# A delta-rule attention layer with an 8-expert MoE: block inverses from 16x16 halves, VectorE transposes, and expert tiles of 256 rows

## The reference

```python
kb = k * beta[..., None]
att = jnp.where(tri, 0.0, -(kb @ jnp.swapaxes(k, -1, -2)))        # strictly lower, 32 x 32 a chunk
for i in range(1, chunk):                                         # the inverse of I - att, row by row
    upd = jnp.einsum('bhnj,bhnjk->bhnk', att[..., i, :], att)
    att = att.at[..., i, :i].add(upd[..., :i])
att = att + jnp.eye(chunk)
u, w = att @ v, att @ kb                                          # v is beta * v
def step(S, xs):                                                  # over the chunks
    u_adj = u_i - w_i @ S
    o_i = q_i @ S + local @ u_adj
    return S + jnp.swapaxes(k_i, -1, -2) @ u_adj, o_i
...
gout = x @ Wgate + bgate                                          # top 2 of 8 experts
z = (x @ W1 + b1) * (x @ W2 + b2)                                 # 128 -> 256
g = z @ Wg + bg                                                   # 256 -> 256
o = g * sigmoid(g) * (z @ Wl + bl)
y = o @ W3 + b3                                                   # 256 -> 128
return x + attention + sum of the two experts' y by their shares
```

## Time and profile before

| | us |
|---|---|
| median of 3 runs (lowest to highest) | 948.98 (945.25 to 949.86) |
| the profiled execution | 941.82 |
| its span, first to last instruction | 939.9 |
| PE busy / PE weight loads | 674.9 / 524.2 |
| DVE busy | 677.4 |
| POOL busy | 467.7 |
| ACT busy | 272.5 |
| DMA | 113.04 MB, 120 GB/s over the span |
| mean granted clock of PE | 0.791 |

### The profile page before, as it was taken

One profiled execution on the slowest core, in us unless ns is written; L12 is line 12 of the kernel. 1 busy time (PEld: TensorE's weight loads), 2 busy tenths in 40 slices (PEclk: granted clock), 3 DMA queues, 4 the chain that ended last, 5 costly groups with the idle time before them and its releaser, 6 DMA issues.

```text
span 939.9 us, 33031 instructions
## 1 busy us (share of the span) xinstructions
PE 674.9 (72%) x14332; PEld 524.2 (56%) x14332; DVE 677.4 (72%) x1432; ACT 272.5 (29%) x489; POOL 467.7 (50%) x526
## 2 busy tenths in 40 slices
PE   3762855757886879589877787777888887676651
PEld 3552853546564656467666565656666575555531
DVE  5769988876955898678658895897477973894241
ACT  2432113241342234222522332233144223113020
POOL 2622137782444556335824783274723257753635
PEclk9855557798977898777978899899796987566575
DMA  9765545374315223701531537326542124213121
GB/s 346 277 249 195 166 159 190 107 201 128 101 26 156 87 81 82 153 26 58 175 114 41 138 109 211 99 59 155 109 106 81 43 87 104 78 49 105 34 71 56
DMA packets 87598, 113.04 MB, mean 120 GB/s; under 512 B 57312, under 2 KB 62432, under 8 KB 83360
## 3 DMA queue, kind: packets, MB, share of 16 engines
q0 software_dynamic: 11616, 51.03, 18.8%
q1 hardware_dynamic: 68720, 37.50, 14.5%
q10 hardware_dynamic: 7120, 22.42, 6.7%
HBM read 77.63 MB, written 34.90 MB: 120 GB/s over the span
## 4 chain that ended last, share of the span: by engine, by line
PE 34%; DVE 26%; issue 16%; POOL 10%; DMA 5%; SPq 4%; ACT 4%; ACTq 1%; DVEq 0%; POOLq 0%
PE ps_shared L1581 6%; DVE solve_prod L1435 5%; PE ps_shared L1737 4%; PE ps_shared L1799 4%; PE ps_g L1577 3%; SPq L842 3%; PE ps_l L1577 3%; DVE solve_T L1442 3%; POOL xs L994 3%; PE ps_shared L1577 3%; PE ps_shared L1716 2%; PE ps_shared L1586 2%; DMA solve_L<-system_d 2%; DVE acc L1364 2%; PE ps_x L1577 2%
## 5 line engine op out<-in xcount | busy, mean ns | idle before, releaser
L1435 DVE TENSOR_TENSOR solve_prod<-solve_T,solve_L 128x2 f32<-128x2 f32 (+30 forms) x248 | 129.7, 523 | 35.7 <-DMA solve_L<-system_d 29.8
L994 POOL DMA_INDIRECT xs<-xn_d,owner_i x92 | 91.7, 997 | 50.5 <-issue 24.9
L1060 POOL TENSOR_TENSOR z<-work,z 128x512 fp32r<-128x512 f32 x46 | 59.5, 1294 | 98.7 <-ACT z L1229 98.4
L1442 DVE TENSOR_REDUCE solve_T<-solve_prod 128x1 f32<-128x2 f32 (+30 forms) x248 | 101.0, 407 | 6.2
L1577 PE MATMUL ps_x<-xr,w_up 128*128 128x512 f32 x276 | 94.8, 459 | 7.3 <-DVE work L1544 4.4
L1577 PE MATMUL ps_g<-z,w_mid 128*128 128x512 f32 x276 | 85.2, 448 | 10.5 <-DVE work L1548 5.6
L1577 PE MATMUL ps_l<-z,w_mid 128*128 128x512 f32 x276 | 79.4, 425 | 0.2 <-DVE work L1553 0.2
L1026 POOL DMA_INDIRECT w_mid<-y_d,slot_i x64 | 63.4, 991 | 18.4 <-issue 17.9
L1799 PE MATMUL ps_shared<-w_mid,work 128*128 128x128 f32 x368 | 56.3, 317 | 21.9 <-DVE work L1553 18.2
L1577 PEld LDWEIGHTS ps_g<-z,w_mid 128*128 128x128 f32 x276 | 55.8, 210 | 28.4 <-issue 13.2
L1737 PE MATMUL ps_shared<-head_vs,taps 32*32 32x16 f32 x4096 | 54.9, 196 | 20.3 <-issue 19.3
(11 more groups left out here) (246 smaller groups left out, 1428.5 us busy)
## 6 DMA issues: line engine op xcount, KB each, us to landing
mid_d<-w_mid ACTq DMA_DIRECT2D x8, 1024.0 KB, 5.8
work<-expert_weights ACTq DMA_DIRECT2D x16, 384.0 KB, 4.4
y_d<-work SPq DMA_DIRECT2D x23, 256.0 KB, 2.2
xa_d<-xr SPq DMA_DIRECT2D x8, 512.0 KB, 6.7
xa<-xa_d SPq DMA_DIRECT2D x8, 512.0 KB, 4.3
up_d<-w_up ACTq DMA_DIRECT2D x8, 512.0 KB, 3.0
solve_L<-system_d SPq DMA_DIRECT2D x64, 64.0 KB
system_d<-masked SPq DMA_DIRECT2D x8, 256.0 KB, 3.4
```

What stands on the lines that cost most here:

```text
L994: pool.indirect_dma_start(xs[par][:, c, :], None, xn_d.rearrange("w p (c d) -> (w p c) d", c=CPW), bass.IndirectOffsetOnAxis(owner_i[:, w ...
L1060: pool.tensor_tensor(low[:, :], up1[i], high[:, :].bitcast(FP), ALU.subtract).then_inc(S["z_low"], 1)
L1435: seq.mark(dve.tensor_tensor(prod, solve_T[:, 0:k, 0:i + 1], over(solve_L[:, i, 0:i + 1].unsqueeze(1), P, k, i + 1), ALU.mult))
L1442: made = dve.tensor_reduce(solve_T[:, 0:k, i], prod, AX.X, ALU.add, negate=True)
```

## The change

1. **The solve** takes only the two 16 x 16 triangles on the diagonal of each block, 128 of them on 128 partitions: 15 steps of i x i elements. `solve_in` is 8 DMAs of 16 x 16 x 16, `inverse_out` is 1 DMA, `inv` is 8 DMAs into `parts`, a block-diagonal tile. Two new stages make the lower left quarter, -D2 x L x D1 in the block's terms: `low` (PE, 64 small products of 16 columns; DVE transposes `parts` into `parts_T`; ACT copies the product to `low_part` with a scale of -1 or 0 by partition), and `full` (PE, 64 small products; DVE copies the first 16 columns of `parts` to `inverse` and adds the product to the other 16). `system` on POOL, `eye` and the diagonal are gone. `u` waits for `full`.
2. **Beta and router rows** are turned by one DVE transpose a window of 32 x 32 blocks (`by_step`); ACT takes the sigmoid from there; `rank` is 4 additions of 32 partitions. ACT's copy, the 64 one-column products and the router's 4 transposes on PE are gone. Wgate is laid out for each of the four heads.
3. **Experts** in tiles of 256 rows: the formula for TILES gives 39 instead of 23 (9984 slots, not 11776). Both halves j share one bank, 256 columns each, and a stage does both: 36 matmuls of 256 columns a tile as before of 512, `down` 4 fp32 products (8 before), 2 row gathers and 2 transposes (4 before). `load_up` and `load_mid` are one each a tile as before, so 39 each. DVE's and ACT's bias steps are two of 128 x 256 a stage; `zlow` and ACT's copy of z stay 128 x 512, one a tile. The load streams are split in even and odd tiles.
4. `FLOW` and `PULL` are set anew, so the order of the work changes everywhere.

```diff
-TILE = 512
+TILE = 256
 TILES = (2 * SEQS * STEPS + EXPERTS * (TILE - 1)) // TILE
 SLOTS = TILES * TILE
 CHUNKS = WINDOWS * CPW
-LANES = TILES * CPW
+CPT = TILE // P
+LANES = TILES * CPT
+MOST = SEQS * STEPS // TILE
 MARK = 8
...
-        return [[(DVE_, 0.1 + min(i, KH) * (i + 1) / 900)]]
+        return [[(DVE_, 0.14 + i * i / 900)]]
...
-        yield need(("solve_in", w, 0))
-        for i in range(1, CHUNK):
+        yield need(("masks0", 0, 0), ("solve_in", w, 0))
+        for i in range(1, KH):
             yield "solve_mul", w, i, None
             yield "solve_sum", w, i, None
         if w >= 2:
...
         yield need(("inverse_out", w, 0))
         if w == 0:
             yield "fold", 0, 0, None
+        yield "inv", w, 0, None
         if w:
             yield need(("w_T", w - 1, 1))
-        yield "inv", w, 0, None
+        bk = yield TAKE
+        yield "low", w, 0, bk
+        leave(bk, "low", w + 1)
+        bk = yield TAKE
+        yield "full", w, 0, bk
+        leave(bk, "full", w + 1)
         yield need(("v_b", w, 0), ("k_T", w, 0))
         if w >= 1:
...
-        yield need(("own", 0, 0) if kind == "load_xs" else ("image_out", EXPERTS - 1, 0), ("place", 0, 0))
-        for t in range(TILES):
+    def expert_loads(kind, par, behind):
...
+                elif name == "inv":
+                    sp.wait_ge(S["in_inverse"], 16 * (w + 1))
+                    sp.wait_ge(S["masked"], 1)
+                    if w:
+                        sp.wait_ge(S["full"], w)
+                        sp.wait_ge(S["low_ps"], w)
+                        sp.wait_ge(S["parts_T"], w)
                     for half in range(2):
-                        sp.dma_start(inverse_d[par, :, KH * half:KH * half + KH, :],
-                                     solve_T[64 * half:64 * half + 64, :, :]).then_inc(S["in_inverse"], 16)
-                elif name == "inv":
-                    sp.wait_ge(S["in_inverse"], 32 * (w + 1))
-                    if w:
-                        sp.wait_ge(S["wT_ps"], w)
-                    for h in range(HEADS):
-                        sp.dma_start(inverse[head_rows(h), :, :],
-                                     inverse_d[par, h * RUNS:h * RUNS + RUNS].rearrange("n k i -> k n i")).then_inc(
-                                         S["in_inv"], 16)
+                        for h in range(HEADS):
+                            first = HD * h + KH * half
+                            sp.dma_start(parts[first:first + KH, :, KH * half:KH * half + KH],
+                                         inverse_d[par, half, h * RUNS:h * RUNS + RUNS].rearrange("n k i -> k n i")).then_inc(
+                                             S["in_inv"], 16)
                 elif name == "x_res":
                     if w:
                         sp.wait_ge(S["in_part"], 16 * w)
                     else:
-                        sp.wait_ge(S["beta_T"], WINDOWS)
...
+                elif name == "beta":
+                    dve.wait_ge(S["rows_ps"], w + 1)
+                    if w >= 2:
+                        dve.wait_ge(S["beta"], w - 1)
+                        dve.wait_ge(S["glog"], w - 1)
+                    dve.transpose(by_step[par], runs_flat(ps[:, :])).then_inc(S["rows"], 1)
...
                 elif name == "solve_mul":
-                    k = min(i, KH)
-                    prod = solve_prod[:, 0:k * (i + 1)].rearrange("p (k j) -> p k j", k=k)
+                    prod = solve_prod[:, 0:i * i].rearrange("p (k j) -> p k j", k=i)
                     if i == 1:
                         dve.wait_ge(S["in_solve"], 16 * SOLVE_LOADS * (w + 1))
-                        dve.wait_ge(S["eye"], w + 1)
+                        dve.wait_ge(S["masked"], 1)
+                        if w:
+                            dve.wait_ge(S["in_inverse"], 16 * w)
                     else:
                         dve.wait_ge(seq.sem, summed_at)
-                    seq.mark(dve.tensor_tensor(prod, solve_T[:, 0:k, 0:i + 1],
-                                               over(solve_L[:, i, 0:i + 1].unsqueeze(1), P, k, i + 1), ALU.mult))
+                    seq.mark(dve.tensor_tensor(prod, solve_T[:, 0:i, 0:i],
+                                               over(solve_L[:, i, 0:i].unsqueeze(1), P, i, i), ALU.mult))
                     product_at = seq.n
                 elif name == "solve_sum":
-                    k = min(i, KH)
-                    prod = solve_prod[:, 0:k * (i + 1)].rearrange("p (k j) -> p k j", k=k)
+                    prod = solve_prod[:, 0:i * i].rearrange("p (k j) -> p k j", k=i)
                     dve.wait_ge(seq.sem, product_at)
-                    made = dve.tensor_reduce(solve_T[:, 0:k, i], prod, AX.X, ALU.add, negate=True)
-                    if i < CHUNK - 1:
+                    made = dve.tensor_reduce(solve_T[:, 0:i, i], prod, AX.X, ALU.add, negate=True)
+                    if i < KH - 1:
...
+                elif name == "low":
+                    dve.wait_ge(S["in_inv"], 16 * SOLVE_LOADS * (w + 1))
+                    if w:
+                        dve.wait_ge(S["full_ps"], w)
+                    dve.transpose(parts_T[:, :, :], parts[:, :, :]).then_inc(S["parts_T"], 1)
+                elif name == "full" and not halfway:
+                    halfway = True
+                    if w:
+                        dve.wait_ge(S["wT_ps"], w)
+                    dve.tensor_copy(inverse[:, :, 0:KH], parts[:, :, 0:KH])
+                elif name == "full":
+                    halfway = False
+                    dve.wait_ge(S["full_ps"], w + 1)
+                    dve.tensor_tensor(inverse[:, :, KH:], ps[:, 0:RUNS * KH].rearrange("p (r i) -> p r i", i=KH), parts[:, :, KH:],
+                                      ALU.add).then_inc(S["full"], 1)
                 elif name == "fir" and i:
                     if i == 1:
...
+                    dve.wait_ge(S["up1"], w + 1)
+                    dve.wait_ge(S["x2"], w + 1)
+                    for j in range(FJ):
+                        own = half(up1[par], j)
+                        made = dve.scalar_tensor_tensor(own, half(ps_x2, j), bias_of(1, w, j), own, ALU.add, ALU.mult)
+                    made.then_inc(S["z"], 1)
...
+                elif name == "low":
+                    pe.wait_ge(S["in_inv"], 16 * SOLVE_LOADS * (w + 1))
+                    pe.wait_ge(S["system_raw"], CPW * (w + 1))
+                    for r in range(RUNS):
+                        for h in range(HEADS):
+                            made = small(ps, KH * r, KH, h, masked[par][head_rows(h), r // SEQS, 0, r % SEQS, :],
+                                         parts[head_rows(h), r, KH:])
+                    made.then_inc(S["low_ps"], 1)
+                elif name == "full":
+                    pe.wait_ge(S["low"], w + 1)
+                    pe.wait_ge(S["parts_T"], w + 1)
+                    for r in range(RUNS):
+                        for h in range(HEADS):
+                            made = small(ps, KH * r, KH, h, parts_T[head_rows(h), r, :], low_part[head_rows(h), r, :])
+                    made.then_inc(S["full_ps"], 1)
                 elif name == "u":
-                    pe.wait_ge(S["in_inv"], 64 * (w + 1))
+                    pe.wait_ge(S["full"], w + 1)
                     pe.wait_ge(S["v_b"], w + 1)
-                    pe.wait_ge(S["k_b"], w + 1)
+                    pe.wait_ge(S["beta_mask"], w + 1)
                     for r in range(RUNS):
                         for h in range(HEADS):
                             made = small(ps, HD * r, HD, h, inverse[head_rows(h), r, :], v_b[par][head_rows(h), r, :])
...
+                elif name in ("mid_g", "mid_l"):
+                    n = int(name == "mid_l")
+                    if n == 0:
...
+                    for j in range(FJ):
+                        for k in range(FJ):
+                            made = product(half((ps_g, ps_l)[n], j), [gl_of(w, part, k, n, j) for part in range(2)],
+                                           [z[par][:, part, k, :] for part in range(2)], start=k == 0, stop=k == FJ - 1)
+                    made.then_inc(S[("g_ps", "l")[n]], 1)
                 elif name == "down":
-                    pe.wait_ge(S["o"], FJ * (w + 1))
-                    for c in range(CPW):
+                    pe.wait_ge(S["o"], w + 1)
+                    for c in range(CPT):
                         for k in range(FJ):
-                            made = pe.matmul(ps[:, c * D:(c + 1) * D], gated[par][k][:, c * P:(c + 1) * P], down_of(w, k),
+                            made = pe.matmul(ps[:, c * D:(c + 1) * D], half(gated[par], k)[:, c * P:(c + 1) * P], down_of(w, k),
                                              start=k == 0, stop=k == FJ - 1)
                     made.then_inc(S["y_ps"], 1)
```

415 lines of the change are left out of this document (193 added, 222 removed).

## The result

| | before | after |
|---|---|---|
| median (lowest to highest), us | 949.38 (945.25 to 949.86) | 979.72 (978.93 to 986.48) |
| profiled span, us | 939.9 | 977.4 |
| PE / DVE / POOL busy, us | 674.9 / 677.4 / 467.7 | 670.5 / 543.2 / 455.8 |
| DMA, MB | 113.04 | 134.56 |
| granted clock | 0.791 | 0.76 |

The changed kernel is slower: ratio 1.0345, 95% interval 1.029 to 1.040. On another chip it ran at 1.0149 (1.009 to 1.0207) of the kernel before, so the loss is 1.5 to 3.5 per cent. There two of its four runs, 975 and 993 us, were in a slower state and don't count, so that ratio rests on runs of 959 and 969 us. The forecast was 871.

A forecast was written before the change was run, and what follows sets the result against it. B was taken as PE work plus waits, half for a DVE 74% full; in C and D a chain decides. 177 + 547 + 52 + 86 = 862 of span, plus 1.9 and 7.2 for the median: 871; range 826 to 925.

The forecast's parts named there:

- A: Stretch from the start to window 0's u, 0 to 217 us before; forecast 177, bounds 165 to 195.
- B: Stretch from window 0's u to window 6's, 217 to 799 us before; forecast 547, bounds 510 to 600.
- C: Stretch from window 6's u to window 7's, 799 to 854 us before; forecast 52, bounds 45 to 60.
- D: Tail after window 7's u, 854 to 940 us before, without solve or experts; forecast unchanged at 86.
- Behind the solve: Path from the solve's output issue to u's products: 7.2 us before, forecast 15, or 16 with a SyncE queue gap.
- Experts: Expert matmuls in B: 256 columns cost 0.54 of 512, nothing gained or lost, -17 to +50 us at the ends.
- Rival 3: Short expert matmuls cost 0.66: B +50, time 921; slower than before from 0.73 on; chance 0.08, 0.02 for that end.
- PE busy in B: TensorE's work in B: 467.7 - 6 - 1 + 23 = 483 us.
- The clock: TensorE's granted clock in B rises from 0.86 to 0.90 with fewer gaps, taken as worth 15 us.
- Idle in B: TensorE's idle time in B: 31 for DVE, 25 issue, 15 rest, 8 new hand-offs, 79 us; 114 before.
- Rival 1: PE's waits for DVE in B are a chain's and stay: B 597, time 921; chance 0.20.
- Rival 4: Expert weight loads with two buffers set the tile's beat; at 17 us B is 629, time 953; chance 0.06.

The follow-up runs named there:

- all three at once: Changed kernel, own order, with low and full products for one run only, half the expert weight bytes and one load for the solve's input: 887.1 us, 0.934.
- Few products: Changed kernel, own order, with low and full products of the last run alone, 4 instead of 64 in each: 940.63 us, 0.9912.
- half the weights: Changed kernel, own order, with half the bytes in each expert weight load, 0.89 MB a tile instead of 1.78: 939.42 us, 0.9919.
- the same new order: Kernel before laid out anew by its planner with trace durations and a searched preference table, first order: 1.0025; slower chip 1.0017.

## Why the prediction was wrong

It forecast 871 and faster; the kernel is 1.5 to 3.5 per cent slower. Of the 115 us of span that are missing, A has 13, B 86 (68 of idle time, 15 of clock, 3 of work), C 14 and D 2.

- *The solve's own steps*: right. 38.9 + 28.7 = 67.6 us, where 68 were said. *Small products' busy time*: right, 28.4 against 30.
- *Behind the solve*, 15 us, "hand-offs 0.5": mis-sized. Window 0's solve ends at 160.0 and its inverse is complete at 185.3: 25. Some 7 us of it are the two stalls inside low and full, the loads start 4.4 us after the output is issued (2.2 in window 7 before), and the eight loads land 3.4 us behind their last issue.
- *Stretch A*, 177: 190. The solve ended 25 us after it began, as forecast; 12 of the 13 us are the path behind it, with u itself. With the stalls and traffic cut (all three at once) A is 175.
- *Experts*, ratio 0.54: right, 0.166 / 0.315 = 0.53. Rival 3 and its far end fall. On the line through the 81 and 131 ns of the Trainium skill (TensorE: Matmul & The Clock Gate, Back-to-back issue gap) the ratio would be 0.75, an estimate; the trace doesn't agree, at 0.53. DVE's pairs were dearer than the 838 ns I took from a plain product: each half takes 475, a pair 950 (L1585, L1578 and L1572 alike), so the split costs 0.2 a pair and not 0.09, 24 us in all. That part of an instruction's time is fixed, as the Trainium skill has it (VectorE: DVE Perf Modes, The TRN2 errata), agrees with the trace, 950 for two halves against 745; how much of the 24 us PE waited for isn't separated.
- *PE busy in B*, 483: right, 486. *The clock*, 15 us: didn't come; it was 0.83 and not 0.90, beside 147 us of gaps where 79 were forecast.
- *Idle in B*, 79: this is the step that failed; it is 147. Two of its terms were wrong. Of the 61 us that DVE released I kept 31, "since its load falls"; it is 58. DVE's load did fall, by 86 us, but load was not what the waits hung on: in the new order DVE stands for the solve's loads, whose trip takes 9.2 to 15.6 us where the order was laid for 7.1, and one load in place of eight gave 12 us back. Of the 37 of "issue" I kept 25, while the change adds 1500 instruction pairs to PE and 28 MB to the queues from which it is supplied; it is 63. That row was in front of me, with "issue" as its largest line, and I priced low and full at the busy time of their like, though a group of the like has its own row of waits: L1581 in the earlier trace rows has 11.0 us of issue beside its 15.2 of work. Few products and half the weights, 22 us less each, are the two cuts at this term, and both went with shorter issue waits.
- *C*, 52: 66; *D*, 86: 88. "With 30 steps it is done long before" held the order of the triangles fixed, and it moved.
- *Rival 1* had the mechanism nearest to it: PE's waits stay, and DVE's did, 58 against 61. It was too small, as it didn't let issue grow. *Rival 4*, weight loading as the tile's beat, is not what happened: the loads land in 7.4 us, PE waits 7.7 us for them in B. But 35 MB less gave 22 us, with PE's issue waits 21 us shorter, and that no rival had; what the 28 MB more of the change cost by themselves wasn't measured.

## What to carry to other kernels

A group of small instructions costs its supply too: put the "issue" idle of the like beside its busy time, and look at what the change adds to the DMA queues in the same stretch. Where engines run fixed lists, work that is taken off one engine only pays if the list doesn't send it to its next wait early: check the landings that the order was laid with against the trace, before and not after the table of preferences is tuned. And a part can't be judged in one order; two orders of the same stages were up to 1.6 per cent apart, and the kernel before needs new orders of its own to be compared with.

## What the runs showed of the hardware

PE's instructions come in packets of 16 KB on queue q8, one for about 127 matmuls with their weight loads. In streams of small products PE stops there, for 1.4 us in the middle and 5.7 at most (54 stops, 88.8 us in the changed kernel), and starts again 1.1 to 1.7 us after a packet has ended. With half the expert weights, at equal instructions, it is 49 stops and 60.2 us.

Two of the chips run the kernel before in 1009 us and not 947. The same kernel in the same new order has 130 issue waits with 140 us on one of them and 54 with 94 us on an ordinary one, and PE's busy time is 692 against 678. The waits that came are of another kind: those that end with a packet are 36 with 56 us there and 43 with 64 us here, the others 94 with 83 us against 11 with 30. Of those 94, 53 take 0.40 to 0.56 us, a length that none of the ordinary chip's 11 has. What they are stays open. The largest issue line on the slower chip, then the same line on the ordinary one (total us, times, longest):

```profile
PE ps_shared L1584 <- issue: 64.1, 82, 6.5
```

```profile
PE ps_shared L1584 <- issue: 31.6, 20, 6.3
```

The one load that replaces eight is issued in 0.33 us, eight gathering ones in 3.8 to 6.3, and the solve step that waits for them starts up to 5.9 us later.
